# One step of an LSTM on VectorE: the output gate's sum placed ahead of the other gates' products

## The reference

```python
def step(carry, xp_t):
    prev_h, prev_c = carry
    h_bar = xp_t + prev_h @ Wh
    i = jax.nn.sigmoid(h_bar[:, 0:Hdim])
    f = jax.nn.sigmoid(h_bar[:, Hdim:2 * Hdim])
    o = jax.nn.sigmoid(h_bar[:, 2 * Hdim:3 * Hdim])
    g = jnp.tanh(h_bar[:, 3 * Hdim:4 * Hdim])
    next_c = f * prev_c + i * g
    next_h = o * jnp.tanh(next_c)
    return ((next_h, next_c), next_h)
```

## Time and profile before

| | |
|---|---|
| median of 3 runs | 1120.87 us |
| span of the profiled execution | 1121.8 us |
| busy: TensorE matmul / weight load | 97% / 88% |
| busy: VectorE, ScalarE, GpSimd | 72%, 52%, 35% |
| the LSTM's steps | 45.7 to 702 us of the span |

### The profile page before, as it was taken

The page is one execution under the profiler, slowest core; times in us unless marked ns, Lnnn a source line. Parts: engine busy times, 40 slices in busy tenths (PEclk is TensorE's granted clock), DMA queues, the critical chain, the costliest instruction groups (busy, mean ns, idle before and its releaser), DMA issues. The chain is left out here.

```text
span 1121.8 us, 55238 instructions
## 1 busy us (share of the span) xinstructions
PE 1084.2 (97%) x21946; PEld 984.9 (88%) x21946; DVE 809.2 (72%) x3458; ACT 588.7 (52%) x2147; POOL 398.2 (35%) x1373
## 2 busy tenths in 40 slices
PE   6789999999999999999999999899999999999998
PEld 5779999999999999999999987688888888888877
DVE  6567777777777777777777776786666666676697
ACT  4355666666665666566566553433333333334486
POOL 3645555545555555555555430290000000000041
PEclk9758999999999999999999999899999999999999
DMA  8312202101101200000001110000000000000022
GB/s 257 88 32 60 61 23 60 60 24 59 60 25 58 60 23 23 14 23 24 13 4 26 15 15 14 2 2 1 2 2 2 1 2 2 1 4 2 4 89 81
DMA packets 54918, 36.94 MB, mean 33 GB/s; under 512 B 25560, under 2 KB 53514, under 8 KB 54668
## 3 DMA queue, kind: packets, MB, share of 16 engines
q1 hardware_dynamic: 54060, 33.12, 10.4%
q10 hardware_dynamic: 608, 0.30, 0.1%
HBM read 28.42 MB, written 4.98 MB: 30 GB/s over the span
## 5 line engine op out<-in xcount | busy, mean ns | idle before, releaser
L605 ACT ACTIVATE gel<-bank,seq 128x256 f32<-128x256 f32 x256 | 121.7, 475 | 214.6 <-PE bank L1247 210.9
L1245 PE MATMUL bank<-XHL,WE 128*128 128x256 f16 x768 | 210.2, 274 | 7.3 <-DVE XHL L836 3.5
L1245 PE MATMUL bank<-GH,WE 128*128 128x256 f16 x768 | 209.6, 273 | 1.5 <-DVE GH L862 0.9
L1247 PE MATMUL bank<-XHL,WE 128*128 128x256 f16 x768 | 210.1, 274 | 0.0
L1246 PE MATMUL bank<-XHL,WE 128*128 128x256 f16 x768 | 210.0, 273 | 0.0
L1247 PE MATMUL bank<-GH,WE 128*128 128x256 f16 x768 | 209.7, 273 | 0.0
L1246 PE MATMUL bank<-GH,WE 128*128 128x256 f16 x768 | 209.6, 273 | 0.0
L1357 PE MATMUL bank<-LH,seq 128*128 128x16 f16 x6144 | 194.8, 170 | 9.5 <-DVE LH L902 9.1
L1357 PEld LDWEIGHTS bank<-LH,seq 128*128 128x128 f16 x6144 | 171.7, 96 | 28.4 <-DVE LH L902 13.4
L1247 PE MATMUL bank<-seq 128*128 128x64 f16 (+2 forms) x1088 | 164.9, 208 | 0.0
L1246 PE MATMUL bank<-seq 128*128 128x64 f16 (+2 forms) x1088 | 163.6, 208 | 0.0
(11 more groups left out here) (211 smaller groups left out, 2776.4 us busy)
## 6 DMA issues: line engine op xcount, KB each, us to landing
stage<-in_L_cond_ew SPq DMA_DIRECT2D x64, 128.0 KB, 2.2
stage<-in_L_cond_W SPq DMA_DIRECT2D x32, 256.0 KB, 3.6
XHL<-in_x SPq DMA_DIRECT2D x8, 512.0 KB, 9.2
out<-WE SPq DMA_DIRECT2D x16, 256.0 KB, 2.1
stage<-in_L_cond_sw SPq DMA_DIRECT2D x2, 1024.0 KB, 5.3
scratch<-rows SPq DMA_DIRECT2D x96, 8.0 KB, 2.3
stage<-in_L_cond_Wx SPq DMA_DIRECT2D x1, 1024.0 KB, 9.4
stage<-in_L_cond_Wh SPq DMA_DIRECT2D x1, 1024.0 KB, 11.5
```

The source lines that it names most:

```text
L605: nc.scalar.activation(gel[:, m % 2, :], banks[m % len(banks)][:, 0:256], ACT.Gelu_apprx_tanh, scale=scale, bias=bias).then_inc(s["a_g"], 1)
L1245: MM(out_, w(HI), x(HI), start=start, stop=False, skip_group_check=True)
L1247: return MM(out_, w(HI), x(LO), start=False, stop=stop, skip_group_check=True)
```

## The change

The waits for `pe_o` and the reduction into `oz` are moved ahead of the wait for `a_fig` and the two products. Nothing is added or taken away, and no other engine's stream is touched.

```diff
                 x = X[:, :, :, bass.ds(blk * U + u, 1)].rearrange("p c b o -> p (c b o)")
+                dve.wait_ge(s["pe_o"], n + 1)
+                V.reduce_sum(oz[:], OB[u // G][:, :].rearrange("p (a m t b) -> p m t b a", a=2, m=C, t=G)[:, :, u % G],
+                             AX_X).then_inc(s["v_oz"], 1)
                 dve.wait_ge(s["a_fig"], n + 1)
                 if n:
                     dve.wait_ge(s["v_c2"], n)
                 V.scalar_tensor_tensor(fc[:], tf, 1.0, c2[:], ALU.add, ALU.mult)
                 V.scalar_tensor_tensor(ig[:], ti, 1.0, tg, ALU.add, ALU.mult).then_inc(s["v_ig"], 1)
-                dve.wait_ge(s["pe_o"], n + 1)
-                V.reduce_sum(oz[:], OB[u // G][:, :].rearrange("p (a m t b) -> p m t b a", a=2, m=C, t=G)[:, :, u % G],
-                             AX_X).then_inc(s["v_oz"], 1)
                 dve.wait_ge(s["v_ig"], n + 1)
                 V.scalar_tensor_tensor(c2[:], fc[:], 0.5, ig[:], ALU.mult, ALU.add).then_inc(s["v_c2"], 1)
```

## The result

| | kernel before | changed kernel |
|---|---|---|
| median of the runs | 1120.92 us (1120.48 to 1122.87, 4 runs) | 1129.16 us (1128.43 to 1130.25, 4 runs) |
| ratio, 95% interval | | 1.0066 [1.0052, 1.0079] |
| span of the profiled execution | 1121.8 us | 1126.6 us |
| VectorE busy | 72% | 74% |

The changed kernel is slower by 8.2 us. The forecast was +3.5 (1124.4) with a range up to 1128.0: the direction was right, the size was not. The chosen mechanism has to be looked at first, since it may be right and something else missing.

A forecast was written before the change was run, and what follows sets the result against it. The ring of dependences through `hh`, not TensorE's work, was taken to set the step; 2.8 + 0.1 + 0.6 + 0.3 = +3.8 us gave 1124.7, lowered to 1124.4, range 1119.8 to 1128.0 (the forecast's own 1122.4 to 1127).

The forecast's parts named there:

- (a) to (d): The u = 4 step laid out anew: `oz` first, `fc` 0.13 behind it, `tc` 0.017 longer and ending 0.022 later.
- Rival 1: Level: longer durations are only how the profiler records an idle start; 1119.5 to 1122.5 us; chance 0.25.
- Rival 2: Faster: `fc` follows `oz` after 0.10, so the output arm's 0.04 is all won; 1118.4 us; chance 0.10.
- rival 3: Slower still: `fc` is held until `oz` has ended, 0.09 more per step; 1144 us; chance 0.02.
- Rival 4: `ig` and `c2` fall on GpSimd operations in half of the steps, +5 more; 1129 us; chance 0.07.
- (f): Six steps in which `fc` waited for VectorE itself, not `tfig`: `fc` moves back 0.13, +0.10 each, +0.6 us.
- ordinary step: 202 LSTM steps, each 0.022 longer less 0.008 from unstretched `fc`, so 0.014 each: +2.8 us.
- u = 1 steps: 14 steps before the last block lose 0.13 to 0.15; at most 0.03 each gets through: +0.3 us.

The follow-up runs named there:

- second profile of before: The kernel before run once more without any edit, for a second profile: 1121.82 us, 0.9999 [0.9989, 1.0009], span 1119.5.
- the new order with the half sum: Changed kernel with the output gate's sum over the first feature half only, the other half left zero: 1123.01 us, 1.0007 against the kernel before.

## Why the prediction was off

**The mechanism held.** `oz` starts 0.04 behind TensorE, `fc` stands behind `oz`, `ig` 0.10 behind `fc`, `c2` 0.22 behind `ig`, `tc` 0.03 behind `c2`, `to` waits for nothing in the end, the load 0.05 behind `hh`: all as laid out in (a) to (d), read above in one step and true in the medians. Rival 1 (level) said that the longer durations are only how a start on an idle engine is recorded. `tc` is 229 ns in all 256 steps and `hh` still follows its end by 0.03 (medians 0.033 and 0.032), so the length is real delay. Rival 2 needed `fc` 0.10 behind `oz`; it is 0.14. For rival 3 `fc` would have had to wait for `oz`'s end, 0.22. The Trainium skill has, beside the rule that I weighed, a second section in "VectorE: DVE Perf Modes", "Two Vector instructions with no wait between them": only an instruction that is held waits until all earlier ones have finished. That goes with the 0.14 behind a reduction of 0.22. Rival 4 saw `c2` and `ig` on GpSimd operations in half of the steps; `c2` is 191 ns in the median, so they are not. That the measured time is rival 4's 1129 is chance.

**The sum by its own terms.** The steps of the two traces, subtracted one by one, in us. The first column is against the profile on which the prediction rests, the second against the second profile of before:

| term | forecast | first | second |
|---|---|---|---|
| ordinary steps, u = 9 among them (210) | 2.9 | 3.8 | 4.7 |
| VectorE late, the six steps of (f) | 0.6 | 0.7 | 0.7 |
| u = 1 steps | 0.3 | -0.3 | -0.2 |
| stalls of the stream (six steps) | none | 1.6 | 1.6 |
| the first two steps, and steps with room | none | 0.1 | 0.5 |
| ahead of the stage | none | -2.1 | -0.5 |
| behind the stage | none | 1.0 | 0.5 |
| sum = difference of spans (rounded) | 3.8 | 4.8 | 7.2 |

Two rows hide something. The six steps of (f) met their 0.6 by luck: 0.3 of the 0.7 is step 16 alone, where `hh` ends only 0.02 later. What differs is TensorE's granted clock, whose mean over this step (PEclk, the 0.63 and 0.86 below) was lower. It rose from 0.50 to 1.00 2.3 us after the step's start in the changed kernel, 0.7 us in the second profile of before and 1.0 in the first. The step in the changed kernel and in the second profile of before:

```profile
87.41:90.44 3.03, 3.03 (x80) 3.03 (x78) 1.68 (x11) 1.06 (x4) 1.12 (x5) 0.63 0.30 91
```
```profile
86.98:89.67 2.69, 2.69 (x81) 2.66 (x79) 1.15 (x8) 0.86 (x4) 1.16 (x5) 0.86 0.19 45
```

Step 17, a u = 1 step, gave 0.2 of this back, which is most of the fall in the row of the u = 1 steps; the other thirteen changed by less than 0.1 together, so the +0.3 forecast for them was wrong. Of the other five steps of (f) three paid 0.10 as forecast, the u = 15 step 0.05 and the u = 8 step 0.02. The 0.5 of the first two steps in the last column goes with the clock too: it rose 2.6 us after the first load in the second profile of before and 5.1 us after it in the changed kernel.

**The step that failed** is the last one, the sum. It has three faults.

First, its main term was mis-sized: 0.014 per ordinary step was 0.018 against the same profile and 0.022 against the second. The spacing behind `oz` was taken as 0.133 from an `oz` in a close row, and the earlier trace rows, where `rz` does start on an idle VectorE, was read as 0.13 though its own starts say 0.14 (48.91 to 49.05); an `oz` that starts on an idle VectorE lasts 224 ns in the median instead of 213 and lets `fc` follow after 0.141. I had this effect in hand for `c2` and `tc` and did not apply it to `oz`. The bound I gave, 0.14, was right. Against this `tc` became longer by 0.014 (215 to 229) and not by 0.017. The step from 0.018 to 0.022 is that in the second profile of before `tc` lasted 213 ns instead of 215 and `oz`, which holds `tc` up there, 211 instead of 213. In all the term came out 1.8 us above its 2.9 in the second column.

Second, a term was missing: six stalls, 1.6 us, from where the products now stand in VectorE's instruction stream. No row of before showed such a stall on the ring, so it could not be read there.

Third, "the same on the runs' median, which differs from it by 0.9 us only" took the profile for a usual execution. It differed from the runs in more than that, since a run is its span plus 1.8 us: the profile was 2.7 us longer than the median run. The difference of the spans is 4.8 us on the first profile and 7.2 on the second: 2.4 us that no term could have held. With the usual execution as base the same kernel pair differs by 7.2 in span and the timed medians by 8.2 and 7.6.

**What stays open.** Behind the stage the changed kernel is 0.5 to 1.0 us longer. TensorE's granted clock fell to its low level there, 1.0 us behind the last step's load in the changed kernel, 2.3 and 5.2 in the two profiles of before. The first 5 us after the last step's load, first profile of before, second profile of before, changed kernel:

```profile
699.30:704.30 5.00, 2.23 (x53) 1.80 (x53) 3.26 (x16) 0.60 (x3) 0.00 (x0) 1.00 0.00 0
```
```profile
696.40:701.40 5.00, 2.23 (x51) 1.75 (x52) 3.26 (x16) 0.60 (x3) 0.00 (x0) 0.73 0.00 0
```
```profile
703.10:708.10 5.00, 2.13 (x49) 1.53 (x50) 2.96 (x16) 0.71 (x3) 0.00 (x0) 0.60 0.00 0
```

The rest of the program from that load on took 422.5, 423.1 and 423.5 us. The second is the unchanged kernel, so this is not the change's own doing, at least not alone. All twelve profiles are ordered alike: three with full clock in that stretch (before, the new order with the half sum, and the sum left out where there is room) had 422.5 to 422.7, two with a mean of 0.73 and 0.76 had 423.1, and seven with 0.53 to 0.62 had 423.4 to 423.7. So the tail's length goes with the fall of the clock. Whether the new order makes the early fall more likely was not settled.

## What to carry to other kernels

When a ring through several engines sets the step, an instruction put ahead of the ring's member costs the spacing that it forces, less the time by which it can start early. It pays only if the arm it serves is late by more than that. Taking work out of a gap on an engine also makes the next instruction there start idle, and it then lasts longer; apply this to the moved instruction too. Compare the profiled execution with the timed runs (span plus the constant offset) before its steps are counted as the base.

## What the runs showed of the hardware

An instruction of 128 x 32 values that finds its engine idle lasts longer than in a close row: `tc` on ScalarE 229 ns against 213 to 215, `c2` on VectorE 191 against 181, `oz` (64 values read) 224 against 213. And this is real time for whoever waits: the next engine follows the end by the same 0.03. VectorE lets the next instruction start 0.10 us after a product has started, 0.11 after a reduction of 32 values and 0.14 after one of 64 (0.134 where the reduction stood in a close row, 0.141 where the engine had been idle), before the reduction has ended. VectorE loses 0.23 to 0.29 us at certain places of its instruction stream, a multiple of 128 recorded instructions apart, and six more instructions at the start move the places; it is seen only where the late instruction is `fc` or `ig` in a close row, and an 8 KB instruction packet starts 0.7 to 1.0 us after it. The same program had TensorE's granted clock rise or fall at moments that differ by some us between executions; one late rise cost a step 0.3 us, an early fall behind the last step up to 1.1.
